# First layer's experts: three of four batches sorted by expert into blocks of 128 rows

## The chip, the cores and the metric

The kernel runs on one core of a Trainium2 chip. The metric is the time on the device in microseconds (us). The engines are called by the profile's names: PE (TensorE's matmuls, PEld its weight loads), DVE (VectorE), ACT (ScalarE), POOL (GpSimd) and SP (SyncE, which issues DMAs here).

## The reference, cut to what matters

Two layers, each an attention-like part and an expert part with gated residuals. What the change touches is the expert part of the first layer, on 4 batches of 1024 tokens of 128 values:

```python
E, FFN, TOP_K = 8, 176, 2
scores = softmax(xt @ gate_w.T)
topk_w, topk_idx = top_k(scores, TOP_K)
topk_w = topk_w / (sum(topk_w) + 1e-20)
combine = zeros((T, E)); combine[t, topk_idx] = topk_w
for e in range(E):
    g, u = split(xt @ w1[e], 2, axis=-1)
    out = out + combine[:, e:e + 1] * (silu(g) * u @ w2[e])
```

So each token needs two of eight experts; the reference computes all eight and weights six of them with zero.

## The kernel before

The program is a sequence of blocks: attention (16 groups, one for each batch and key head), the first layer's experts, a selective scan, and the second layer's experts with slots of a fixed capacity. A block ends for all engines together, and its last output is needed by the next block's normalization.

`experts` follows one list of steps, made by `experts_plan` (from line 1287 on); each engine walks through the same list and takes from it what is its own, so the list is the order of every queue. The 4096 tokens lie in 8 chunks of 512, and the 8 x 176 = 1408 hidden columns in 11 pieces of 128 (`NC`). One unit ("up", k) is a chunk and a piece: on PE six float32r matmuls of 512 columns (high and low parts, lines 1475 to 1477, for both halves of w1) and one that spreads the combine weights over the piece's rows (line 1484); on ACT a silu (1717), on DVE two products (1633, 1638). The step ("down", k) stands two units later (`LAG`) and adds four fp32 matmuls of 128 columns (1494), each of which the trace shows as two records. So all eight experts are computed for every token, and the combine weights, transposed and spread, do the choosing. A chunk's result is scaled by DVE (1647), added by POOL (1765) and its row statistics are taken by DVE.

Between the units stand the steps of preparation: "norm" (POOL), "ln" (transposes on PE, ACT), "score" (PE, 1442), "route" and "weights" (some twenty short DVE operations each, from 1511 and 1543 on), "tr" (the combine weights' transposes), "w" (the split of w1 into parts, in batch 0's first units), and steps for the next layer ("mod", "norm2", "ln2", "tap"). Ahead of the first unit are the output projection of attention's last batch ("out", 1414) and the routing of chunk 0. SP loads the weights at the start of the block.

The second layer's experts, `capacity_experts`, already send token rows to slots in memory (an indirect DMA from POOL, 1251), fetch them (SP, 2622), store results (2627) and gather them back (POOL, 2594); its gathers use four semaphores for each of the two choices.

Of the kernel before, what the change touches and what calls it, by code (L numbers as in the profile page):

```python
# [7 lines left out]
F32 = mybir.dt.float32  # L8
F32R = mybir.dt.float32r
I32 = mybir.dt.int32  # L10
# [445 lines left out]
def attention(nc, sems, a, h_t, attn_t, wo, ident, eps, zeros, stats, mv, mod_t, gates, slots_in, slots_zero):  # L456
# [3 lines left out]
    with ExitStack() as ctx:  # L460
# [526 lines left out]
        def sync(e):  # L987
# [6 lines left out]
            for step in plan:  # L994
# [30 lines left out]
                elif kind == "v" and key[0] in (1, 2):  # L1025
# [3 lines left out]
                                zeros[:, :, :].to_broadcast([P, E1 * CAPACITY // P, HID])).then_inc(slots_zero, 16)  # L1029
# [244 lines left out]
PHASES = ((0, 1), (1, 4), (4, NCHUNK))  # L1274


NORMED_AT = {1: (0, 0), 2: (0, 2), 3: (0, 4), 4: (1, 1), 5: (1, 6), 6: (2, 1), 7: (2, 6)}
CHOSEN_AT = {1: (0, 6), 2: (3, 1)}
MOD_AT = ((4, 2), (4, 5), (5, 2))

NEXT_AT = (((4, 4), (4, 7)), ((4, 9), (5, 3)))


def experts_plan():


    behind = {}

    def put(n, c, *steps):
        behind.setdefault(n * NC + c, []).extend(steps)  # L1290

    for n, (m, c) in NORMED_AT.items():
        put(m, c, ("norm", n))
        put(m, c + 1, ("ln", n))
        put(m, c + 2, ("score", n))
    for p, (m, c) in CHOSEN_AT.items():
        put(m, c, ("route", p))
        put(m, c + 1, ("rstd", 1) if p == 1 else ("rstd2",), ("exp", p))
        put(m, c + 2, ("weights", p))
    for n in range(1, NCHUNK):  # L1300
        put(n - 1, NC - 2, ("tr", n))
    for j, (m, c) in enumerate(MOD_AT):
        put(m, c, ("mod", j))
    for n, (rows_at, columns_at) in enumerate(NEXT_AT):
        put(*rows_at, ("norm2", n))
        put(*columns_at, ("ln2", n))
    put(NCHUNK - 1, 4, ("tap", 0))
    for c in range(NC - 3):
        put(0, c, ("w", c + 3))
# [3 lines left out]
    for k in range(NCHUNK * NC):  # L1313
        plan.append(("up", k))
        if k >= LAG:
            plan.append(("down", k - LAG))
        if k % NC == LAG + 1 and k > NC:
            plan.append(("stats", k // NC - 1))
        plan += behind.get(k, [])
    plan += [("down", k) for k in range(NCHUNK * NC - LAG, NCHUNK * NC)]  # L1320
    plan.append(("stats", NCHUNK - 1))
# [3 lines left out]
def experts(nc, sems, a, x, x_again, attn_t, wo, stats, mv, mod_t, gates, gate, iota, ident, eps, slots_zero, h_t, later, later_in,  # L1325
# [1448 lines left out]
```

## Time and profile before

| | us |
|---|---|
| median of 3 runs | 1877.63 (1877.07 to 1878.2) |
| profiled execution | 1874.3 |
| its span in the trace | 1872.6 |
| PE busy | 1552.5 (83% of the span) |
| DVE busy | 1187.0 (63%) |
| POOL busy | 1264.9 (68%) |
| ACT busy | 791.1 (42%) |

All times of rows are us from the start of the span. Busy shares are averages over stages with different limits, so they don't tell what a change in one stage is worth: that is read from stretches of that stage and from its timeline. A matmul's duration in a row is the time until its result is out, and matmuls overlap, so a rate is read from the distance between starts. The clock column is the granted clock of PE as a share of 2.4 GHz, where 1.00 is 2.4 and 0.50 is 1.2 GHz.

### The profile page before, as it was taken

The page shows a single profiled execution, that of the slowest core. Times are in us where ns is not written, and L with a number is a line of the kernel's source. Part 1 is how long each engine was busy: PE and PEld are TensorE (multiplying, and loading weights), DVE is VectorE, ACT ScalarE, POOL GpSimd, SP SyncE. Part 2 cuts the span into 40 slices and gives each one's busy share as a digit, 9 for nine tenths or more (in the row PEclk, how much of TensorE's full clock was granted, in tenths as well). Part 3 has the DMA queues.
Part 4 walks back from the last instruction along what each step waited for, and adds up shares of the span by engine and source line. Part 5 has one row for each costly group of instructions (what it writes and reads, how often), then busy time and mean ns, then how long its engine had stood idle before and what let it go on. Part 6 is the DMA issues. An engine that isn't in the chain of part 4 may idle for free. (4 is left out here: it accounts for less than half of the span.)

```text
span 1872.6 us, 26570 instructions
## 1 busy us (share of the span) xinstructions
PE 1552.5 (83%) x8882; PEld 1072.4 (57%) x8882; DVE 1187.0 (63%) x2509; ACT 791.1 (42%) x1347; POOL 1264.9 (68%) x1073
## 2 busy tenths in 40 slices
PE   5799999999999999999999989999965664356970
PEld 3455556755656765567656568888831231235970
DVE  6866676576666567666666235576659989952134
ACT  2245444344443354443444433322267855423320
POOL 5588998798888788887888753110026667658476
PEclk7799999999999999999999999999978876667995
DMA  6333322221122122122121020000036555405333
GB/s 176 70 80 79 69 56 47 46 68 35 40 63 69 29 52 68 35 52 63 35 58 45 12 67 1 1 1 1 1 101 157 143 124 139 115 26 173 98 93 85
DMA packets 93560, 125.30 MB, mean 67 GB/s; under 512 B 13664, under 2 KB 53492, under 8 KB 93424
## 3 DMA queue, kind: packets, MB, share of 16 engines
q1 hardware_dynamic: 89328, 115.58, 24.9%
q0 software_dynamic: 4096, 8.02, 1.5%
q8 instruction: 72, 1.18, 0.3%
q14 instruction: 64, 0.52, 0.1%
HBM read 56.56 MB, written 16.78 MB: 39 GB/s over the span
## 5 line engine op out<-in xcount | busy, mean ns | idle before, releaser
L838 DVE CUSTOM_DVE_ANT_0 ring<-ring,mask 128x128 f32<-128x128 f32 (+7 forms) x512 | 383.7, 769 | 186.0 <-PE ring L700 185.6
L924 ACT ACTIVATE prob<-ring 128x512 f32<-128x512 f32 x576 | 315.1, 597 | 296.6 <-PE ring L715 293.0
L978 POOL TENSOR_TENSOR acc<-acc,prob 128x512 f32<-128x512 f32 x272 | 353.3, 1299 | 72.1 <-ACT prob L924 48.3
L731 PE MATMUL ps_o<-prob,v 128*64 128x256 f32 x2304 | 282.0, 386 | 4.2 <-issue 3.8
L700 PE MATMUL ring<-k,x 128*128 128x512 f32 (+3 forms) x768 | 250.0, 405 | 36.4 <-ACT prob L924 22.1
L714 PE MATMUL ring<-x,k 128*128 128x512 f32 x576 | 258.6, 449 | 24.5 <-DVE neg_m L838 15.4
L715 PE MATMUL ring<-x,k 128*128 128x512 f32 x576 | 229.2, 398 | 0.0
L700 PEld LDWEIGHTS ring<-k,x 128*128 128x128 f32 x768 | 136.6, 197 | 143.9 <-ACT prob L924 50.5
L731 PEld LDWEIGHTS ps_o<-prob,v 128*64 128x64 f32 x2304 | 154.2, 137 | 106.3 <-issue 38.5
L975 POOL TENSOR_TENSOR acc<-prob 128x512 f32<-128x512 f32 x144 | 184.4, 1281 | 8.8 <-ACT prob L924 7.4
L945 POOL TENSOR_TENSOR other<-other,sin 128x512 f32<-128x512 f32 x96 | 136.3, 1420 | 57.1 <-DVE other L817 56.6
L714 PEld LDWEIGHTS ring<-x,k 128*128 128x128 f32 x576 | 109.3, 190 | 99.4 <-issue 44.0
L2375 POOL TENSOR_TENSOR m_hc<-m_st,m_crep 128x1024 f32<-128x1024 f32 x42 | 98.8, 2353 | 53.6 <-DVE m_st L2140 47.9
L947 POOL TENSOR_TENSOR rot<-rot,other 128x512 f32<-128x512 f32 x96 | 129.1, 1344 | 7.5
L1765 POOL TENSOR_TENSOR first_h<-first_h,e_scaled 128x512 f32<-128x512 f32 x8 | 10.3, 1285 | 174.4 <-DVE e_scaled L1647 174.4
L715 PEld LDWEIGHTS ring<-x,k 128*128 128x128 f32 x576 | 110.0, 191 | 19.9 <-issue 7.3
L830 DVE TENSOR_TENSOR rot<-rot,other 128x512 fp32r<-128x512 f32 x64 | 73.2, 1143 | 69.5 <-ACT other L906 69.5
L1633 DVE TENSOR_TENSOR e_both<-e_silu,ps_moe 128x512 f32<-128x512 f32 x88 | 60.4, 687 | 87.9 <-PE ps_moe L1477 69.4
L1717 ACT ACTIVATE e_silu<-ps_moe 128x512 f32<-128x512 f32 x88 | 52.6, 598 | 134.9 <-PE ps_moe L1477 132.2
L963 POOL TENSOR_SCALAR_AFFINE_SELECT prob<-prob 128x512 f32<-128x512 f32 x128 | 91.4, 714 | 25.8 <-ACT prob L924 24.7
L816 DVE TENSOR_TENSOR rot<-ring,cos 128x512 f32<-128x512 f32 x96 | 66.3, 690 | 58.1 <-PE ring L682 57.7
L2594 POOL DMA_INDIRECT c_got<-slots_out,f_slot x64 | 66.5, 1040 | 45.7 <-issue 39.8
(322 smaller groups left out, 3068.5 us busy)
## 6 DMA issues: line engine op xcount, KB each, us to landing
x<-other SPq DMA_DIRECT2D x256, 128.0 KB, 2.3
m_x_rep<-u_mem SPq DMA_DIRECT2D x59, 512.0 KB, 4.6
x<-rot SPq DMA_DIRECT2D x128, 128.0 KB, 2.3
slots_in<-zeros SPq DMA_DIRECT2D x2, 2048.0 KB, 8.7
slots_out<-wo SPq DMA_DIRECT2D x16, 256.0 KB, 2.5
gate<-slots_in SPq DMA_DIRECT2D x11, 256.0 KB, 3.2
m_x_rep<-u_mem SPq DMA_DIRECT2D x10, 256.0 KB, 4.2
e_w<-in_w SPq DMA_DIRECT2D x3, 704.0 KB, 6.9
```

The source lines that it names most:

```text
L700: mm = e.matmul(ps[:, c0:c1], x1[g % 2][:, h, qs], k1[g % 3][:, c0:c1], start=True, stop=True)
L714: e.matmul(banks(step, BANK), k1[g % 3][:, ks], x1[g % 2][:, :, qs], start=True, stop=False)
L715: e.matmul(banks(step, BANK), k2[g % 3][:, ks], x2[g % 2][:, :, qs], start=False, stop=True).then_inc(s2_pe.sem, 1)
L731: mm = e.matmul(ps_o[s * D:(s + 1) * D, qb % 2 * 2 * P:(qb % 2 + 1) * 2 * P], v[g % 2][:, kb, :], prob[i % NPROB][:, s * 2 * P:(s + 1) * 2 ...
L838: e.tensor_tensor_reduce(ps, ps, mask_1[:, SEQ - n:SEQ], 1.0, -3.0 * NEG, ALU.add, ALU.min, neg_m[g % 2][:, c, h, qb % QPC:qb % QPC + 1]). ...
L924: e.activation(prob[i % NPROB][:, :], banks(("s2",) + key, BANK), ACT.Exp, scale=-1.0).then_inc(s2_exp.sem, 1)
L945: e.tensor_tensor(other[i][:, :], other[i][:, :], sin[:, cc], ALU.mult).then_inc(rotated.sem, 1)
L947: e.tensor_tensor(rot[i][:, :], rot[i][:, :], other[i][:, :], ALU.add).then_inc(rotated.sem, 1)
L963: e.affine_select(tile[:, :], tile[:, :], [[0, G], [1, P]], ALU.is_ge, 0.0, base=0, channel_multiplier=-1).then_inc(causal.sem, 1)
L975: e.tensor_tensor(total[:, :], first[:, :], tile[:, :], ALU.add).then_inc(summed.sem, 1)
L978: e.tensor_tensor(total[:, :], total[:, :], tile[:, :], ALU.add).then_inc(summed.sem, 1)
L2375: e.tensor_tensor(hc[(b * NG + g) % NHC][:, :], st[r][:, :], crep[b % 2][:, :], ALU.mult).then_inc(hc_pool.sem, 1)
```

## The change

Batch 0 stays as it is: 22 units. Batches 1 to 3 are computed by choice of expert:

- For each of these batches DVE counts the tokens of each expert, PE forms running counts ("rank"), and DVE computes for both choices of every token a slot so that each expert's tokens start at a multiple of 128 ("place"), and a table with the expert of each of 24 blocks of 128 rows (`NBLOCK` = 16 + 8, enough for any distribution).
- PE loads the table's 24 values into registers ("regs"); the plan holds this step four times, twice for batch 2.
- The normalized rows are transposed back to token order ("back"), stored with the token's weight as a 129th value, and sent by POOL to their slots in memory, 16 indirect DMAs a batch ("send").
- SP fetches sets of 512 sorted rows; PE transposes them ("xt"), ACT and DVE split them. A step ("sup", q) computes a pair of blocks: for each block three float32r matmuls whose stationary side is the 128 rows and whose moving side is the 2 x 176 columns of the block's expert, at an address from a register. ACT takes the silu, DVE multiplies with weight and other half, PE transposes ("htr"), ACT copies, and "dn" multiplies by the expert's w2, again at a register's address. DVE scales, SP stores.
- POOL gathers each token's two results by indirect DMAs that add into x, 16 a batch, the second choice after the first eight have landed.
- In attention SP writes zeros to the three buffers of sorted rows. The wait for the gate's weights also covers a table and a constant, one of them issued behind the other weights.
- The final stage's gathers have two semaphores for each choice instead of four, since semaphores are short.

```diff
+                elif kind == "v" and key[0] in (3, 4, 5):
+
+                    e.dma_start(sorted_in[key[0] - 3].rearrange("(s p) n -> p s n", p=P),
+                                zeros[:, :, :].to_broadcast([P, NBLOCK, HID + 1])).then_inc(slots_zero, 16)
...
+DENSE = SEQ // BANK
+UNITS0 = DENSE * NC
+NBLOCK = 2 * TPB + E0
+SETS, PAIRS = NBLOCK // 4, NBLOCK // 2
...
+PHASES = ((0, 1), (1, 2), (2, 4), (4, 6), (6, 8))
...
+CHOSEN_AT = {1: 2, 2: 7, 3: 12}
...
+        if p >= 2:
+            put(k + 2, ("count", p - 1))
+            put(k + 3, ("rank", p - 1))
+            put(k + 4, ("place", p - 1))
+            put(k + 6, ("regs", p - 1))
...
+    for m, k in enumerate((12, 14, 17, 19)):
+        put(k, ("send", 1, 2 * m), ("send", 1, 2 * m + 1))
+    put(21, ("send", 2, 0), ("send", 2, 1))
+    for m, q in enumerate((1, 4, 7)):
+        put_among(q, ("send", 2, 2 * m + 2), ("send", 2, 2 * m + 3))
+    for m, q in enumerate((9, 12, 15, 17)):
+        put_among(q, ("send", 3, 2 * m), ("send", 3, 2 * m + 1))
...
+    put_among(4, ("score", 7), ("back", 7), ("stats", 1), ("mod", 0))
+    put_among(5, ("route", 4), ("exp", 4))
+    put_among(6, ("weights", 4), ("count", 3), ("rank", 3), ("place", 3))
+    put_among(8, ("regs", 2), ("mod", 1))
+    put_among(10, ("mod", 2))
...
+    put_among(19, ("regs", 3))
+    put_among(28, ("tap", 0))
+    for m, q in enumerate((20, 23, 26, 29)):
+        put_among(q, ("gather", 1, m))
+    for m, q in enumerate((32, 35)):
+        put_among(q, ("gather", 2, m))
...
+    plan.append(("xt", 0))
+    for q in range(pairs):
+        plan.append(("sup", q))
+        if q < 2:
+            plan.append(("down", UNITS0 - LAG + q))
+        if q % 2 and q + 1 < pairs:
+            plan.append(("xt", q // 2 + 1))
+        if q >= 1:
+            plan.append(("htr", q - 1))
+        if q >= 2:
+            plan.append(("dn", q - 2))
+        plan += among.get(q, [])
+        if q == 31:
+            plan.append(("sum", 1))
+    plan += [("htr", pairs - 1), ("dn", pairs - 2), ("dn", pairs - 1)]
+    plan += [("gather", 2, 2), ("gather", 2, 3), ("sum", 2)]
+    plan += [("gather", 3, m) for m in range(4)] + [("sum", 3)]
...
+                elif kind == "regs":
+                    b = step[1]
+                    e.wait_ge(placed, placed0 + b)
+                    _, expert[b] = nc.values_load_multi_w_load_instructions(
+                        of[0:1, b - 1, :], engines=[mybir.EngineType.PE], min_val=0, max_val=(E0 - 1) * F0,
...
+                elif kind == "xt":
+                    e.wait_ge(*rows_had(k))
+                    for j in range(4):
+                        mm = e.transpose(bank[:, j * P:(j + 1) * P], rows_of(k)[:, j, 0:HID], ident[:, :])
+                    mm.then_inc(xt_pe, 1)
+                elif kind == "sup":
+                    q = step[1]
+                    b, block, i = q // PAIRS + 1, 2 * (q % PAIRS), q // 2 % 2
+                    if q % 2 == 0:
+                        e.wait_ge(xt_dve, xt_dve0 + q // 2 + 1)
+                    if q < 2:
+                        e.wait_ge(both_dve, UNITS0 - 1 + q)
+                    else:
+                        e.wait_ge(hid_dve, UNITS0 + q - 1)
+                    for j in range(2):
+                        cols, to = slice((2 * (q % 2) + j) * P, (2 * (q % 2) + j + 1) * P), ps_up[q % 2][:, j, 0:2 * F0]
+                        at = bass.ds(expert[b][block + j], F0)
+                        e.matmul(to, xt_hi[i][:, cols], w_hi[:, :, at], start=True, stop=False)
+                        e.matmul(to, xt_hi[i][:, cols], w_lo[:, :, at], start=False, stop=False)
+                        mm = e.matmul(to, xt_lo[i][:, cols], w_hi[:, :, at], start=False, stop=True)
+                    mm.then_inc(up1_pe, 1)
+                elif kind == "htr":
+                    e.wait_ge(hid_dve, UNITS0 + k + 1)
+                    for j in range(4):
+                        mm = e.transpose(bank[0:HALF, j * P:(j + 1) * P], both[k % 2][:, j * HALF:(j + 1) * HALF], ident[:, :])
+                    mm.then_inc(htr_pe, 1)
+                elif kind == "dn":
+                    q = step[1]
+                    b, block = q // PAIRS + 1, 2 * (q % PAIRS)
+                    e.wait_ge(ht_act, q + 1)
+                    e.wait_ge(scale_dve, DENSE + q)
+                    for j in range(2):
+                        at, to = bass.ds(expert[b][block + j], HID), ps_dn[:, 2 * (q % 2) + j, :]
+                        for m in range(2):
+                            mm = e.matmul(to, hid[q % 2][0:HALF, (2 * j + m) * P:(2 * j + m + 1) * P], w2s[0:HALF, m, at], start=m == 0, stop=m == 1)
+                    mm.then_inc(dn_pe, 1)
...
+                elif kind == "xt":
+                    n = step[1]
+                    e.wait_ge(xt_act, xt_act0 + n + 1)
+                    e.tensor_tensor(xt_lo[n % 2][:, :], ps_c[turn[step] % 2], xt_hi[n % 2][:, :].bitcast(F32), ALU.subtract).then_inc(xt_dve, 1)
+                elif kind == "sup":
+                    q = step[1]
+                    e.wait_ge(silu_act, UNITS0 + q + 1)
+                    if q >= 2:
+                        e.wait_ge(htr_pe, q - 1)
+                    for j in range(2):
+                        cols = slice(j * F0, (j + 1) * F0)
+                        t = e.scalar_tensor_tensor(both[q % 2][:, cols], silu[q % 2][:, cols], rows_of(q // 2)[:, 2 * (q % 2) + j, HID:HID + 1],
+                                                   ps_up[q % 2][:, j, F0:2 * F0], ALU.mult, ALU.mult)
+                    t.then_inc(hid_dve, 1)
+                elif kind == "dn":
+                    q = step[1]
+                    b, n = q // PAIRS + 1, q // 2
+                    e.wait_ge(dn_pe, UNITS0 + q + 1)
+                    if n >= 2:
+                        e.wait_ge(res_out[n % 2][0], res_out[n % 2][1] + n // 2 * 16)
+                    half = slice(2 * (q % 2), 2 * (q % 2) + 2)
+                    e.tensor_tensor(hid[2 + n % 2][:, :].rearrange("p (j n) -> p j n", n=HID)[:, half, :], ps_dn[:, half, :],
+                                    gates[0][1][:, b:b + 1, :].to_broadcast([P, 2, HID]), ALU.mult).then_inc(scale_dve, 1)
...
+                if kind == "send":
+                    _, b, i = step
+                    if i % 2 == 0:
+                        e.wait_ge(up1_pe, begun)
+                    if i == 0:
+                        e.wait_ge(placed, placed0 + b)
+                        e.wait_ge(tok_act, tok0 + 4 * b)
+                        if b > 2:
+                            e.wait_ge(*all_sent(b - 2))
+                    for k in range(2):
+                        e.indirect_dma_start(sorted_in[b - 1][:, :], bass.IndirectOffsetOnAxis(ap=slot[:, b - 1, k * TPB + i:k * TPB + i + 1], axis=0),
+                                             tok[b % 2][k][:, i, :], None, bounds_check=NBLOCK * P - 1, oob_is_err=False).then_inc(sent[b % 2], 16)
+                elif kind == "gather":
+                    _, b, m = step
+                    if begun < UNITS0 + pairs - 1:
+                        e.wait_ge(up1_pe, begun)
+                    if m == 0:
+                        for r, base in res_out:
+                            e.wait_ge(r, base + b * SETS // 2 * 16)
+                    if m == 0 and b > 2:
+                        e.wait_ge(got[b % 2], (b - 1) // 2 * 2 * TPB * 16)
+                    if m == 2:
+                        e.wait_ge(got[b % 2], ((b - 1) // 2 * 2 + 1) * TPB * 16)
+                    for i in range(4 * (m % 2), 4 * (m % 2) + 4):
+                        e.indirect_dma_start(x[:, b * TPB + i, :], None, sorted_out[b - 1][:, :],
+                                             bass.IndirectOffsetOnAxis(ap=slot[:, b - 1, m // 2 * TPB + i:m // 2 * TPB + i + 1], axis=0),
+                                             bounds_check=NBLOCK * P - 1, oob_is_err=True, compute_op=ALU.add).then_inc(got[b % 2], 16)
...
+            for j in range(2):
+                e.dma_start(w2s[0:HALF, j, :].rearrange("p (e f) -> p e f", f=F0)[:, :, 0:HID],
+                            a["w2_0"][:, j * HALF:(j + 1) * HALF, :].rearrange("e p n -> p e n")).then_inc(w2_in, 16)
+            e.dma_start(blocks[:, :], a["blocks"][0:1, :]).then_inc(gate_in, 16)
...
+            def fetch(n):
+                b, at = n // SETS + 1, n % SETS * BANK
+                if n % SETS == 0:
+                    e.wait_ge(*all_sent(b))
+                if n >= 3:
+                    e.wait_ge(hid_dve, UNITS0 + 2 * n - 4)
+                    e.wait_ge(xt_pe, xt_pe0 + n - 2)
+                e.dma_start(rows_of(n)[:, :, :], sorted_in[b - 1][at:at + BANK, :].rearrange("(s p) n -> p s n", p=P)).then_inc(sorted_done[n % 3][0], 16)
+
+            def store(n):
+                b, at = n // SETS + 1, n % SETS * BANK
+                e.wait_ge(scale_dve, DENSE + 2 * n + 2)
+                e.dma_start(sorted_out[b - 1][at:at + BANK, :].rearrange("(s p) n -> p s n", p=P),
+                            hid[2 + n % 2][:, :].rearrange("p (j n) -> p j n", n=HID)).then_inc(res_out[n % 2][0], 16)
+            sets = (BATCH - 1) * SETS
+            for n in range(2):
+                fetch(n)
+            for n in range(sets):
+                if n + 2 < sets:
+                    fetch(n + 2)
+                store(n)
...
-        gathered0, gathered1 = ([sem(f"gather{k}_{m}") for m in range(4)] for k in range(2))
+        gathered0, gathered1 = ([sem(f"gather{k}_{m}") for m in range(2)] for k in range(2))
```

## Rows read from the trace of the kernel before

**Rows 1.** Stretches: start:end, length, busy us (instructions) by engine, clock, DMA.
```profile
1113.20:1181.60 68.40, 62.34 (x387) 54.58 (x386) 40.02 (x96) 28.71 (x51) 23.81 (x36) 1.00 0.00 1
1181.60:1365.90 184.30, 178.91 (x1093) 156.82 (x1092) 114.13 (x226) 49.94 (x82) 17.17 (x25) 1.00 0.00 1
```

**Rows 2.** Timeline: start, duration, engine, line, tiles, [idle before, releaser].
```profile
1290.47 0.48 PE L1475 MATMUL ps_moe<-e_h_hi,e_w1hi 128*128 128x512 f32 x1
...
1291.72 0.40 PE L1477 MATMUL ps_moe<-e_h_hi,e_w1lo 128*128 128x512 f32 x1
...
1292.19 1.05 PE L1494 MATMUL ps_moe<-e_w,e_hid 128*128 128x128 f32 x8
1293.00 0.48 PE L1475 MATMUL ps_moe<-e_h_hi,e_w1hi 128*128 128x512 f32 x1
...
1292.22 0.69 DVE L1633 TENSOR_TENSOR e_both<-e_silu,ps_moe 128x512 f32<-128x512 f32 x1 [0.94 <-PE ps_moe L1477]
```

**Rows 3.** Timeline, the first up matmul of batch 0.
```profile
1113.25 0.48 PE L1475 MATMUL ps_moe<-e_h_hi,e_w1hi 128*128 128x512 f32 x1
```

**Rows 4.** Timeline of PE, the first unit of batch 1.
```profile
1181.11 0.48 PE L1475 MATMUL ps_moe<-e_h_hi,e_w1hi 128*128 128x512 f32 x1
```

**Rows 5.** Timeline of DVE, end of the stage and start of the next.
```profile
1365.11 0.69 DVE L1647 TENSOR_TENSOR e_scaled<-ps_moe,gate 128x512 f32<-128x512 f32 x1 [1.43 <-PE ps_moe L1494]
...
1368.77 1.33 DVE L2145 COPY m_w_b<-m_w_x 128x128 f32<-128x128 f32 x1 [0.32 <-PEq L1781]
```

**Rows 6.** Timeline: four transposes' loads, eight narrow matmuls, four 16-column loads.
```profile
1103.11 0.47 PEld L1423 LDWEIGHTS ps_moe<-ident,e_xn 128*128 128x128 f32 x4
...
1104.78 1.03 PE L1442 MATMUL ps_route<-gate,e_h 128*128 128x8 f32 x8 [0.96 <-ACT e_h L1691]
...
1112.78 0.42 PEld L1447 LDWEIGHTS ps_moe<-ident,e_comb 128*16 128x16 f32 x4
```

**Rows 7.** The line of the two zero fills in attention.
```profile
L1028 SPq DMA_DIRECT2D slots_in<-zeros x2: 442/442/443, 105.3 to 170.6; - x2
...
DMA to landing us min/median/max: 8.7/8.7/8.7
```

**Rows 8.** The line of the final stage's fetches: issue to landing.
```profile
DMA to landing us min/median/max: 2.7/3.3/4.5
```

**Rows 9.** The line of the final stage's gathers: POOL's register moves, min/median/max ns.
```profile
L2594 POOLq MOVE  x64: 29/29/29, 1767.0 to 1846.1; - x64
```

**Rows 10.** The line of a small load issued behind w1 and w2.
```profile
L1777 SPq DMA_DIRECT2D e_ct<-in_c_t x1: 2624/2624/2624, 1098.5 to 1098.5; - x1
...
DMA to landing us min/median/max: 7.5/7.5/7.5
```

**Rows 11.** Timeline of DVE, the first two operations of one routing.
```profile
1105.85 0.19 DVE L1511 TENSOR_REDUCE e_best<-ps_route 128x4 f32<-128x32 f32 x1 [1.67 <-PE ps_route L1442]
1106.08 0.19 DVE L1513 TENSOR_TENSOR e_less<-ps_route,e_best 128x32 f32<-128x32 f32 x1
```

**Rows 12.** Timeline of POOL, one of the final stage's sends.
```profile
1716.08 0.97 POOL L1251 DMA_INDIRECT slots_in<-attn_t,f_slot  x1 [0.30 <-issue]
```

**Rows 13.** Timeline of POOL, a gather; the DMA view's line of all gathers.
```profile
1777.11 1.00 POOL L2594 DMA_INDIRECT c_got<-slots_out,f_slot  x1 [0.31 <-issue]
...
c_got<-slots_out,f_slot POOLq DMA_INDIRECT x64, 2.6
```

**Rows 14.** Stretches of attention, about one group each.
```profile
170.00:236.00 66.00, 62.51 (x365) 40.20 (x362) 42.91 (x95) 29.53 (x56) 58.06 (x49) 1.00 0.32 81
236.00:301.00 65.00, 60.98 (x358) 39.70 (x357) 42.92 (x96) 29.15 (x55) 58.41 (x50) 1.00 0.22 49
```

**Rows 15.** Stretches of the next stage; a 512-column matmul's load at low clock.
```profile
1440.00:1460.00 20.00, 9.85 (x38) 3.31 (x31) 18.52 (x22) 13.72 (x21) 12.91 (x6) 0.67 0.56 135
1460.00:1480.00 20.00, 16.84 (x71) 8.38 (x69) 19.93 (x37) 16.53 (x17) 13.27 (x8) 0.93 0.58 155
...
1374.42 0.19 PEld L2046 LDWEIGHTS m_ps_w<-attn_t,w_tap 128*128 128x128 f32 x1 [0.24 <-issue]
```

More of the change, by code:

```diff
@@ L1316, in experts_plan, with experts @@
             plan.append(("down", k - LAG))
-        if k % NC == LAG + 1 and k > NC:
-            plan.append(("stats", k // NC - 1))
+        if k == NC + LAG + 1:
+            plan.append(("stats", 0))
         plan += behind.get(k, [])
-    plan += [("down", k) for k in range(NCHUNK * NC - LAG, NCHUNK * NC)]
-    plan.append(("stats", NCHUNK - 1))
+    pairs = (BATCH - 1) * PAIRS
+    plan.append(("xt", 0))
[15 more added lines that the diff above has]
+    plan += [("gather", 3, m) for m in range(4)] + [("sum", 3)]
     return plan
-def experts(nc, sems, a, x, x_again, attn_t, wo, stats, mv, mod_t, gates, gate, iota, ident, eps, slots_zero, h_t, later, later_in,
+def experts(nc, sems, a, x, x_again, attn_t, wo, stats, mv, mod_t, gates, gate, iota, ident, eps, slots_zero, sorted_in, sorted_out, marks, past, h_t, later, later_in,
             cw, w_in, w_tap):
     plan = experts_plan()
-    spare = [step for step in plan if step[0] in ("out", "ln", "tr", "up", "mod", "ln2", "tap")]
+    spare = [step for step in plan if step[0] in ("out", "ln", "tr", "up", "mod", "ln2", "tap", "back", "rank", "xt", "htr")]
     turn = {step: i for i, step in enumerate(spare)}
     shift, scale = 3, 4
+    pairs = (BATCH - 1) * PAIRS
     with ExitStack() as ctx:
@@ L1359, in experts @@
         scaled = [sb(f"scaled{i}", [P, 4, HID]) for i in range(2)]
+        xt_hi, xt_lo = ([sb(f"xt_{n}{i}", [P, BANK], F32R) for i in range(2)] for n in ("hi", "lo"))
+        sorted_rows = [sb(f"sorted{i}", [P, 4, HID + 1]) for i in range(3)]
+        w2s = sb("w2s", [P, 2, E0 * F0])
+        room = attn_t[:, :, :, :].rearrange("p k j n -> p (k j n)")[:, 2 * SEQ:2 * SEQ + 4 * TPB * (HID + 1)]
+        tok = [[room[:, (2 * i + j) * TPB * (HID + 1):(2 * i + j + 1) * TPB * (HID + 1)].rearrange("p (t n) -> p t n", n=HID + 1)
+                for j in range(2)] for i in range(2)]
+        tri, ones, less_one = sb("tri", [P, P]), sb("ones", [P, P]), sb("less_one", [P, P])
+        both_masks, upto, keep, pos = (sb(n, [P, E0, TPB]) for n in ("both_masks", "upto", "keep", "pos"))
+        steps, one, need, end, start = (sb(n, [P, E0]) for n in ("steps", "one", "need", "end", "start"))
+        more, picked, slot_f = sb("more", [P, E0, E0]), sb("picked", [P, 2 * TPB, E0]), sb("slot_f", [P, 2 * TPB])
+        slot = sb("slot", [P, BATCH - 1, 2 * TPB], I32)
+        blocks, over, of_f = sb("blocks", [1, NBLOCK]), sb("over", [1, NBLOCK, E0]), sb("of_f", [1, NBLOCK])
+        of = sb("of", [1, BATCH - 1, NBLOCK], I32)
         ct, sct, wm = sb("ct", [P, BATCH]), sb("sct", [P, BATCH]), sb("wm", [P, 6 * HID])
@@ L1744, in gpsimd @@
                     t.then_inc(norm2_pool, 1)
-                elif kind == "ln":
+                elif kind == "ln" and step[1] < DENSE:
                     n = step[1]
```

247 lines of the change are left out of this document (194 added, 53 removed).

## The prediction

> **What bounds the kernel now.** I read the busy times by stretch first, to find the stage and the engine that sets its pace; then the timeline of one unit; then the stage's entry and exit; then the final stage, because it already has the kinds of transfer that the change adds. In the stretches [rows 1] the experts of the first layer run from 1113.2 to 1368.7. TensorE (PE) is busy 62.3 of 68.4 us and then 178.9 of 184.3 us at a granted clock of 1.00, DVE 62% and GpSimd (POOL) 9% of the second stretch: PE is the bound there, and what is saved on PE shortens the span. One unit (128 of the 1408 hidden columns for 512 tokens) takes 2.52 us in steady state, from 1290.47 to 1293.00: seven 512-column matmuls 0.23 apart (1291.72 to 1292.19 holds two) and eight records of the down step in 0.81 [rows 2]. Batch 0's 22 units begin at 1113.25 and the first unit of batch 1 at 1181.11 [rows 3, 4]; the next block's first work on DVE is at 1368.77 [rows 5]. So 67.9 us stay and 187.7 us are replaced.
>
> **What PE does instead.** Each later batch becomes 24 blocks of 128 rows, 12 pairs, 36 pairs in all. One pair needs 6 up matmuls of 352 columns: 0.23 x 352/512 = 0.16, and since not all of the 0.23 shrinks with the columns 0.166, together 1.00. It needs 4 transposes of the hidden rows and, once in two pairs, 4 of the input; four transposes take 0.47, as in [rows 6], so 0.70. The down step has 4 fp32 matmuls, 8 records at 0.118 (a quarter of the 0.47) = 0.94. Sum 2.65 us a pair if PE waits for nothing, 95 us for 36.
>
> **What sets the pace of a pair.** The rows make a round trip through memory, and SyncE's loop ties it to PE: the fetch of set n+2 stands behind the store of set n-1, which waits for the scaled result of pair 2n-1. From the end of that pair's down step: 0.5 for DVE's scaling (half of a 0.69 op and its wait), 0.45 for issuing the store (0.44 in [rows 7]), 3.3 until the fetch lands [rows 8], so 4.25. PE meanwhile does 2.4 + 1.0 = 3.4 and stands at the transposes of set n+2. After these come 1.9 of PE work until the next such down step, so the loop closes in 6.1 us, 6.3 with the copy and subtraction on ScalarE and DVE: 3.15 us a pair. Bounds: 2.65 (fetch early enough) and 4.0 (below). DVE needs 0.68 + 0.35 + 0.42 plus gaps = 1.6 a pair from its 0.69 per 512 columns [rows 2], ScalarE 1.4; neither binds.
>
> **Register addresses.** The column offset of each expert comes from a PE register; the trace shows no such matmul. Ten of them stand in a pair. A register MOVE on POOL's queue takes 0.029 [rows 9], a whole DMA issue on SyncE 0.44 [rows 7]. With one or two register operations for each, the added time lies between 0.3 and, at 0.1 for each matmul and repeated for each record, 1.4 us. Records with a 16-column load and those with an 8-column moving side both stay at 0.11 to 0.12 apart [rows 6], which looks like the sequencer's own rate, so such operations may not be hidden. The fetch leaves 0.4 a pair of PE idle to hide them; I take 0.3, hence nothing on top of 3.15.
>
> **Loading the registers.** 24 loads, then the same again for the second and third batch, and the plan loads the second batch's twice: four times. At 0.029 a load this is 0.7 us each time, at 0.44 it is 10.6. I take 0.12, near the geometric middle, 2.9 each time, and 1 us of it under matmuls already queued: 4 us in the dense phase, 3 in the sorted one, whose waits hide some. Everything behind it on PE waits, and so DVE and ScalarE. The Trainium skill (Runtime: NRT & Kernel Launch, section Instruction fetch mechanics) gives about 200 ns per register loaded, even in bulk; no run here shows it yet. By that price an estimate is 4.8 us a time and the sum some 7 us more.
>
> **Entry, +3.5.** The wait on the gate's semaphore now asks for four transfers, and the fourth is issued behind w1, w2 and the second copy of w2 (0.72 MB). Before, the small transfer issued behind w2 landed at 1098.49 + 7.5 = 1106.0 while the scores began at 1104.78 [rows 6, 10]. The added 0.72 MB take 2.1 to 2.9 us at 250 to 340 GB/s, so the scores start at about 1108.3. They stand ahead of the second output projection on PE, so all of it counts; bounds 2 and 5.
>
> **Dense phase, +2.8 and +1.** On PE: four transposes back (1.9) and two rank products (1.4), less one transpose (0.4). DVE gets routing and placing for three batches, about 24 us of short operations at 0.22 each, as [rows 11] show, where 22 units leave it 26. They come in bursts of 3 to 6 us, and PE runs ahead of DVE by about 1.9, so most are hidden; 1 us for the rest (bounds -2, since the 2.0 us wait for the combine weights goes, and 6).
>
> **Start of the sorted phase, +5.** The last four sends wait for unit 19, take 0.97 + 0.30 each on POOL [rows 12] and land about 3 later; then the fetch 3.3, transposes 0.5, copy 0.6, subtraction 0.7, while PE has 2.9 units left. The two last down steps are queued behind. Bounds 2 and 8.
>
> **Within it.** 32 pairs at 3.15 are 100.8. DVE's burst at pairs 4 to 6 (routing, counting, placing, about 10 us) exceeds the 1.6 spare a pair plus 1.5 of lead by 4. Scores, transposes and the modulation of the next layer are 7 us of PE, 3 of them uncovered; registers 3. So pair 32 begins at 1181.1 + 3.5 + 3.8 + 4 + 5 + 100.8 + 10 = 1308.2.
>
> **The tail.** PE ends about 15 later. From pair 32 POOL gathers batch 2: 16 indirect DMAs 1.30 apart (1.00 and 0.31 ahead of it) [rows 13], with one landing (2.6) between the halves that add into the same rows: 23.4. Batch 3's 16, 2 landings and the statistics follow: 20.8 + 5.9 + 2.6, then 0.3 for the block's end. With 1 us for accumulation, which the trace does not show, 54 us after pair 32 begins: 1362.2, against 1368.7 (the 1368.77 of [rows 5]). In these last 38 us PE is idle; before, 3.7, from the scaling at 1365.11 on.
>
> **Outside the stage.** Three zero fills of 1.6 MB enter SyncE's queue in attention. The two of 2 MB that are there land in 8.7 and the group periods around them are 65 to 66 us with and without [rows 7, 14], so 0 (bounds 0 and 3). At the end half as many semaphores let eight gathers fly instead of sixteen; a group's landing (2.6) lies under the four issues (5.2) of the next [rows 13], so 0.
>
> **Sum.** 1362.2 - 1368.7 = -6.5; I round to -6. The profiled execution took 1874.3 (span 1872.6), 3.3 below the median 1877.6; so 1868 for a profiled one and 1871.6 for the median.
>
> **Rivals.** (1) The work is PE-bound and registers are cheap: pairs at 2.75 and loads at 0.7 save 13 + 5 us more, 1854. For it: PE needs 2.65, and a fetch landed in 2.7 at best. Against it: the store-before-fetch order. (2) PE's sequencer becomes the bound, the case on the other side: register operations ahead of ten matmuls a pair, at the 0.11 per record that is perhaps already its rate, make a pair 3.8 instead of 3.15, 36 x 0.65 = 23 us more: 1895. It decides from 3.32 us a pair, where the 6 us are gone. (3) Register loads at 0.44 cost 4 x 10.6 instead of 7, with cover some 30 more: 1902. (4) The clock falls: in the next stage, where PE is busy for half to 0.84 of the time, the grant is 0.67 to 0.93 and 512-column matmuls stand 0.43 apart (0.19 and 0.24) [rows 15] instead of 0.23. At that ratio a pair takes 4.9 and the stage 63 more, 1935; half of it, 1903, if it falls in part. For it is that six of sixteen PE steps a pair are transposes; against it, the clock was 1.00 through the first stretch with 9% idle [rows 1]. The skill (TensorE: Matmul & The Clock Gate, section Part 4) says that transposes don't count as PE activity; by it the rival would win, and the trace has no stretch of this mixture to agree or not. (5) The change does not do what it says: 24 blocks are a fixed number, run whether filled or not, so the saving can't fail through the data; I give it 0.
>
> **How the numbers follow.** Forecast 0.46 (1862 to 1881), rival 1 0.14, rival 2 0.22, rival 3 0.11, rival 4 0.05, others 0.02. What a measurement of this kernel can tell from no change is about 0.2%, 3.7 us. Of the forecast's 0.46, 0.32 lies below 1873.9, 0.10 within the band and 0.04 above. Faster: 0.32 + 0.14 + 0.01 = 0.47. Same: 0.10 + 0.02 from rival 2 = 0.12. Slower 0.41. The range runs from 1848, rival 1 with its cheaper bounds, to 1906, which takes in rivals 2 and 3 and leaves rival 4's worse half out.
>
> **What would show it.** Starts of the up matmuls of the sorted phase two pairs apart by 6.3, with PE waiting ahead of the input transposes for a DMA: right. No such wait and gaps named issue: rival 2. A gap on PE of over 3 us ahead of units 14 and 19 and pairs 9 and 20: the loads. Scores at 1108.3; POOL issuing gathers 1.30 apart for 38 us after PE's last matmul; granted clock 1.00 up to there. I am wrong most easily in the pair: each 0.1 us is 3.6.

## The result and the profile after

The changed kernel takes 1904.8 us (median of 4 runs, 1904.5 to 1907.4), the kernel before 1877.35 beside it: ratio 1.0151, 95% interval 1.0133 to 1.0168. The change costs 27.5 us where I forecast a gain of 6. The profiled execution has a span of 1905.7 us, 33.1 more than before.

In stretches (start:end, length, busy us and instructions of PE, PE's loads, DVE, ScalarE, POOL, then clock, DMA share, GB/s), the dense units of batch 0, the 36 pairs, and what comes behind PE's last matmul; they answer to [rows 1]:

```profile
1124.10:1204.10 80.00, 68.12 (x408) 59.07 (x407) 52.94 (x160) 35.42 (x60) 38.58 (x54) 0.96 0.05 15
1204.10:1345.60 141.50, 115.20 (x821) 106.35 (x819) 70.49 (x201) 57.59 (x105) 73.31 (x68) 0.95 0.38 92
1345.60:1399.00 53.40, 0.00 (x0) 0.00 (x0) 4.57 (x32) 0.00 (x0) 37.33 (x24) 0.53 0.26 35
```

PE's busy time fell from 241 to 183 us, but PE now stands still for 12 us in the first stretch, 26 in the second, and all of the third. The waits of PE from 1105 to 1345.6 (engine, tile, line <- who ended the wait: us in all, times, longest):

```profile
PE ps_moe L1562 <- DMA e_sorted<-sorted_in: 11.0, 11, 1.9
PE ps_moe L1550 <- DVE e_upto L1730: 7.3, 2, 5.1
PE ps_route L1540 <- DMA e_blocks<-in_blocks: 6.4, 1, 6.4
PE ps_moe L1576 <- DVE e_xt_lo L1835: 5.0, 13, 1.5
PE ps_moe L1521 <- DVE e_of L1765: 3.3, 1, 3.3
...
PE ps_moe L1635 <- DVE e_of L1765: 2.3, 1, 2.3
```

Four mechanisms are named there: the fetch of the sorted rows (L1562 are the input's transposes), DVE's counting and placing (L1550 is the rank product), the block numbers, and the copy and subtraction behind the transposes.

*Entry* (timeline; answers to [rows 3, 6, 10]):

```profile
1100.64 5.48 SPq L2081 DMA_DIRECT2D e_w2s<-in_w  x2
1106.16 0.41 SPq L2083 DMA_DIRECT2D e_blocks<-in_blocks  x1
1111.94 1.88 PE L1540 MATMUL ps_route<-gate,e_h 128*128 128x8 f32 x8 [6.38 <-DMA e_blocks<-in_blocks]
1113.67 6.50 PE L1512 MATMUL ps_moe<-wo,attn_t 128*128 128x128 f32 x30
1124.15 0.48 PE L1626 MATMUL ps_moe<-e_h_hi,e_w1hi 128*128 128x512 f32 x1
```

SyncE needs 5.48 us to issue the two loads of w2's second copy, so the 24 block numbers are issued only at 1106.16, and PE goes on 5.8 later. The DMA engines are full all the while: from 1100 to 1112 their share, the last number but one, is 1.06.

```profile
1100.00:1112.00 12.00, 5.62 (x51) 5.39 (x50) 1.42 (x7) 2.02 (x4) 0.02 (x1) 0.90 1.06 267
```

The eight narrow score matmuls then take 1.88 us, where [rows 6] have 1.03: PE's clock had fallen while it waited (granted 0.61 from 1112 to 1122). The first expert matmul starts at 1124.15 instead of 1113.25.

*Two undisturbed pairs* (timeline; releaser in brackets):

```profile
1301.24 0.63 PE L1562 MATMUL ps_moe<-ident,e_sorted 128*128 128x128 f32 x4 [0.30 <-DMA e_sorted<-sorted_in]
1303.36 0.42 PE L1576 MATMUL ps_moe<-e_w1hi,e_xt_hi 128*128 x1 [0.16 <-DVE e_xt_lo L1835]
1303.68 0.36 SPq L2100 DMA_DIRECT2D sorted_out<-e_hid  x1
1304.14 0.45 SPq L2095 DMA_DIRECT2D e_sorted<-sorted_in  x1
1305.68 0.41 PE L1576 MATMUL ps_moe<-e_w1hi,e_xt_hi 128*128 x1
1307.43 0.63 PE L1562 MATMUL ps_moe<-ident,e_sorted 128*128 128x128 f32 x4 [0.54 <-DMA e_sorted<-sorted_in]
1309.56 0.42 PE L1576 MATMUL ps_moe<-e_w1hi,e_xt_hi 128*128 x1 [0.17 <-DVE e_xt_lo L1835]
```

From 1303.36 to 1309.56 two pairs take 6.2 us, and PE waits ahead of the input's transposes for the fetch that stands behind the store. Pairs 0, 12, 32 and 34 begin at 1208.19, 1262.65, 1330.14 and 1336.57.

*Tail* (timeline; answers to [rows 5]):

```profile
1388.76 1.56 POOL L2027 DMA_INDIRECT first_h<-sorted_out,e_slot  x1 [0.30 <-issue]
1390.63 1.56 POOL L2027 DMA_INDIRECT first_h<-sorted_out,e_slot  x1 [0.30 <-issue]
1394.01 1.64 DVE L156 BATCH_NORM_STATS2 stats<-first_h 128x6 f32<-128x128 f32 x8 [29.85 <-DMA first_h<-sorted_out,e_slot]
1395.68 0.64 DVE L160 BATCH_NORM_AGGREGATE mv<-stats 128x2 f32<-128x6 f32 x8
1399.07 1.34 DVE L2474 COPY m_w_b<-m_w_x 128x128 f32<-128x128 f32 x1 [2.74 <-PEq L2110]
```

A gather that adds into its rows takes 1.56 us and the next comes 1.86 behind it, not 1.30 as in [rows 13]. The next block's DVE work, at 1368.77 before, starts at 1399.07: 30.3 of the 33.1 us.

### The profile page after: what moved, and what is told of

The parts are those of the page before. It is cut to its first block and busy times, and to the rows that moved or that the text cites. A ratio compares the mean times of both kernels' runs of the same rounds, so it can differ in the third digit from the quotient of the medians.

```text
span 1905.7 us, 26684 instructions
## 1 busy us (share of the span) xinstructions
PE 1500.2 (79%) x8630; PEld 1028.2 (54%) x8630; DVE 1158.4 (61%) x2573; ACT 805.4 (42%) x1379; POOL 1375.1 (72%) x1162
## 5 line engine op out<-in xcount | busy, mean ns | idle before, releaser
L2027 POOL DMA_INDIRECT first_h<-sorted_out,e_slot x48 | 74.9, 1561 | 33.7 <-PE ps_moe L1578 13.7
L743 PE MATMUL ps_l<-acc,v_one 128*64 128x256 f32 x576 | 87.2, 380 | 2.9 <-POOL acc L978 2.9
L1255 POOL DMA_INDIRECT slots_in<-attn_t,f_slot x64 | 63.7, 995 | 32.9 <-issue 14.9
```

## The experiments

Ratios are to the kernel before, run beside each. The changed kernel's is 1.0151 (1.0133 to 1.0168); marks in a trace are more exact for single steps.

**The entry.**

```diff
             e.dma_start(tri[:, :], a["tri"]).then_inc(gate_in, 16)
+            e.dma_start(blocks[:, :], a["blocks"][0:1, :]).then_inc(gate_in, 16)
...
-            e.dma_start(blocks[:, :], a["blocks"][0:1, :]).then_inc(gate_in, 16)
```

> The changed kernel with one transfer moved: the 24 block numbers are fetched right behind the triangle, ahead of w1, instead of behind both copies of w2. Theory A (the entry is set by the place in SyncE's queue: two issues of 2.8 us and 0.72 MB stand ahead of the block numbers, and while PE waits 6.4 us for them its clock falls, so the second output projection takes 10.3 us instead of 7.4): scores start near 1106.4 instead of 1111.9, the projection is back at 7.4, the first expert matmul comes 8 us earlier, median 1904.8 - 8 = 1897. Rival B (the transfers of w1 and w2 fill the DMA engines, and any small transfer lands late beside them, or the weights become the last wait): 0 to 3 us earlier, 1902 to 1905.

Measured: 1894.96 us, ratio 1.0089 (1.006 to 1.0118). Scores at 1107.13, the first expert matmul at 1115.60, 8.5 earlier, with the attention's end 0.7 later: behind it the entry is as long as in the kernel before (18.6 us). Theory A, as far as the place in the queue goes. The transfer now stands ahead of the loads' issues and of their bytes at once, so the run doesn't tell which of the two had made it late.

**Register addresses and loads.**

```diff
-                        at = bass.ds(expert[b][block + j], F0)
+                        fixed = min((block + j) // 3, E0 - 1) * F0
+                        at = slice(fixed, fixed + F0)
...
-                    _, expert[b] = nc.values_load_multi_w_load_instructions(of[0:1, b - 1, :], ...)
+                    expert[b] = None
```

> The changed kernel without register loads and register addresses: each block's matmuls read the columns of a fixed expert (blocks 3e to 3e+2 those of expert e), so the experts' results are not those asked for; all else stays, every wait and matmul included. Theory A (register addresses and loads are hidden: no gap stands at the loads in the dense phase, 0.8 us stands at one in the sorted phase): 0 to 3 us less, median 1902 to 1905. Rival B (the sequencer pays for each addressed matmul, as my second rival had it): 0.3 to 0.65 us less a pair, 11 to 23 less, 1882 to 1894. Rival C (the loads cost about 5 us a time): 10 to 20 less.

Measured: 1899.75 us, ratio 1.0127 (1.0097 to 1.0156). In the trace the step between an even pair and the next odd one, where PE waits for nothing, is 2.31 us with registers and 2.32 without: addressing costs nothing there. It does show where PE's sequencer has been held by a wait. One subtraction and the up matmul that it releases, in the changed kernel and then here:

```profile
1302.53 0.69 DVE L1835 TENSOR_TENSOR e_xt_lo<-ps_moe,e_xt_hi 128x512 fp32r<-128x512 f32 x1 [0.35 <-ACT e_xt_hi L1944]
1303.36 0.42 PE L1576 MATMUL ps_moe<-e_w1hi,e_xt_hi 128*128 x1 [0.16 <-DVE e_xt_lo L1835]
```

```profile
1298.77 0.69 DVE L1835 TENSOR_TENSOR e_xt_lo<-ps_moe,e_xt_hi 128x512 fp32r<-128x512 f32 x1 [0.62 <-ACT e_xt_hi L1944]
1299.51 0.43 PE L1575 MATMUL ps_moe<-e_w1hi,e_xt_hi 128*128 128x352 f32 x1
```

From the end of the subtraction it is 0.14 us with a register address and 0.05 without; over the 18 sets that is some 1.5 us. Where the table is loaded at pair 8 a step shrinks from 4.25 to 3.19. From pair 0 to 32 it gained 4.5 us in all; 1.0 of that is this load and some 1.5 are the addresses. The other 2 are less than the scatter: pairs 12 to 34 took 73.9, 74.0, 76.6 and 79.1 us in four kernels that are alike there, 71.5 here, and PE's waits for the fetch were no shorter (12.6 us against 11.0). What the trace of the changed kernel has for the addresses and loads:

```profile
L1556 PEldq TENSOR_LOAD <-e_of x3: 1689/1806/1964, 1175.7 to 1289.2; - x3
...
L1576 PEldq FUSED_REGOPS  x72: 37/42/42, 1208.1 to 1338.0; - x72
...
L1577 PEldq ALU_OP  x72: 32/32/42, 1208.2 to 1338.1; - x72
...
L1593 PEldq ALU_OP  x72: 32/32/32, 1216.8 to 1344.1; - x72
L1593 PEldq FUSED_REGOPS  x72: 46/51/51, 1216.9 to 1344.3; - x72
```

(Line, queue and operation, count, duration ns min/median/max, first and last start.) All 24 offsets come in one instruction of 1.8 us, three times in all.

> The changed kernel with each of its four steps that load 24 registers done four times over, 96 loads for 24. Theory A (the sequencer runs ahead of the matmuls queued and a load costs 0.03 to 0.05 us: where the step stands in pair 8 of the changed kernel a gap of 0.8 us is named issue, and none stands at units 13 and 18): the pair with the step at 8 grows by 3 us (72 more loads at 0.045), units 13 and 18 by at most 2.5, in all 5 to 9 us more. Rival B (my forecast's 0.12 a load): 8.6 a time, 25 to 35 more. Rival C (0.2 a load, as the Trainium skill has it in Runtime: NRT & Kernel Launch, section Instruction fetch mechanics; no row shows it): 14.4 a time, 50 or more.

The three repeats in front of the last one had no reader, and the built program doesn't contain them: its trace has three TENSOR_LOADs as well, and as many instructions, 26684. So this experiment measured nothing of a load; it is a second measurement of the changed kernel, 1901.6 us (two runs), ratio 1.0123 (1.0105 to 1.014), and shows how far two such measurements lie apart. It also shows that the plan's first load for batch 2, which is done again before use, is not in the program either.

**The gathers.**

```diff
-  bounds_check=NBLOCK * P - 1, oob_is_err=True, compute_op=ALU.add).then_inc(got[b % 2], 16)
+  bounds_check=NBLOCK * P - 1, oob_is_err=True).then_inc(got[b % 2], 16)
```

> The changed kernel with the gathers of the sorted results writing over the rows instead of adding into them (the sums are left out). Theory A (the accumulation is what makes a gather 1.56 us long instead of 1.00): the 24 gathers behind PE's last matmul come 1.30 apart instead of 1.86, 24 x 0.56 = 13.4 less, and 1 from the first half of batch 2: median 1890. Rival B (the length comes from the table read in memory or from where the rows are written): 1.86 apart still, 1905.

Measured: 1887.36 us, ratio 1.0044 (1.0027 to 1.006). Gathers in its trace, then in that of the changed kernel:

```profile
L2027 POOL DMA_INDIRECT first_h<-sorted_out,e_slot x48: 1004/1010/1065, 1283.3 to 1372.7; - x48
...
DMA to landing us min/median/max: 2.5/2.6/3.9
```

```profile
L2027 POOL DMA_INDIRECT first_h<-sorted_out,e_slot x48: 1548/1559/1657, 1287.3 to 1390.6; - x48
...
DMA to landing us min/median/max: 3.2/3.3/4.8
```

From pair 32 (1328.01) to the next block (1381.90) it took 53.9 us, against 68.9 in the changed kernel: the adding is 15 us of the tail. Theory A.

**SyncE's order.**

```diff
-            for n in range(2):
+            for n in range(3):
                 fetch(n)
             for n in range(sets):
-                if n + 2 < sets:
-                    fetch(n + 2)
+                if n + 3 < sets:
+                    fetch(n + 3)
                 store(n)
```

> The changed kernel with SyncE's order turned: the fetch of set n+3 is issued ahead of the store of set n (three fetches first) instead of behind it. Theory A (the loop of store, fetch and transposes makes two pairs 6.3 us where nothing disturbs them): PE's 11 waits ahead of the input transposes, 11.0 us in all, go; two undisturbed pairs take 5.5 to 5.7; from pair 12 to 34 that is 8 to 11 us less, median 1894 to 1897. Rival B (PE's own queue is the bound, through register addresses or through the chain of copy and subtraction behind the transposes): the waits turn into others, two pairs stay above 6.1, 0 to 3 us less.

Measured: 1892.45 us, ratio 1.0075 (1.0048 to 1.0101). Waits of PE from 1260 to 1345.6, of this kernel, then of the changed one:

```profile
PE ps_moe L1576 <- DVE e_xt_lo L1835: 2.2, 10, 0.3
PE ps_moe L1583 <- DVE gate L1786: 1.3, 1, 1.3
PE ps_moe L1593 <- DVE e_hid L1853: 0.7, 1, 0.7
PE ps_moe L1583 <- DVE e_both L1843: 0.5, 1, 0.5
```

```profile
PE ps_moe L1562 <- DMA e_sorted<-sorted_in: 9.4, 10, 1.9
PE ps_moe L1576 <- DVE e_xt_lo L1835: 2.4, 11, 0.8
```

The wait for the fetch is gone, two pairs take 5.5, and pairs 12 to 34 take 62.9 instead of 73.9. Theory A.

**DVE's bursts.** ScalarE copies the ranks out (a copy of 72 columns and a semaphore), and the plan shifts:

```diff
-            put(k + 3, ("rank", p - 1))
-            put(k + 4, ("place", p - 1))
+            put(k + 4, ("rank", p - 1))
+            put(k + 5, ("place", p - 1))
...
-    put_among(6, ("weights", 4), ("count", 3), ("rank", 3), ("place", 3))
+    put_among(6, ("weights", 4), ("count", 3))
+    put_among(7, ("rank", 3), ("place", 3))
```

> The changed kernel with the ranks kept out of PE's way: ScalarE copies them from their bank at once, so that the bank is free before DVE has placed the rows; PE takes the rank products one step later than the routing; and the first of the two loads of batch 2's registers is dropped. Theory A (PE waits behind DVE's bursts: 3.3 and 2.3 us for the bank, 2.2 and 5.1 us for the counts, and its clock falls behind the longest of them): those waits shrink from 12.9 to under 4, another 2 us come from the clock, median 10 lower than the changed kernel, 0.5 point in the ratio. Rival B (DVE's work itself is late, whoever waits for it: the bursts then hold PE at the hidden rows instead): 0 to 3 us lower.

Measured: 1897.35 us, ratio 1.0094 (1.0079 to 1.0109). From the first expert matmul to the last replicating one of the dense units it takes 73.7 us instead of 78.9, from pair 0 to 12 50.1 instead of 54.5: 9.6 together. The start of the sorted phase takes 2.0 of that back, and pairs 12 to 34 took 79.1, with PE's waits for the fetch at 17.7 us; how much of these 5 is scatter I can't tell. Of the four waits behind the bursts (12.9 us) one of 1.9 is left, in front of a rank product: theory A. A new gap of 2.8 us, named issue, stands ahead of unit 14, where the register load now comes right behind the placing.

**Two parts of the change alone, in the kernel before.** The final stage with two semaphores for each choice's gathers instead of four, and the three zero fills in the attention stage:

> The kernel before with one part of the change alone: in the final stage the gathers count on two semaphores for each choice instead of four, so that group m waits for the landing of group m-2. Theory A (my forecast: a group's landing lies under the issues of the next): no change, ratio 1.000. Rival B (the final stage of the changed kernel is 2.3 us longer from its first to its last gather, and this is its price): 2 to 3 us slower, ratio 1.0012 to 1.0016.

> The kernel before with another part of the change alone: the three zero fills of 1.6 MB in the attention stage, to which the first layer's weights wait as they do in the changed kernel. Theory A (my forecast: hidden): no change, ratio 1.000. Rival B (the changed kernel's attention ends 1.7 us later, and the fills are why): 1 to 2 us slower, ratio 1.0005 to 1.001, the last output projection at 1096.3 instead of 1094.6.

Measured: 1877.21 us, ratio 0.9993 (0.9984 to 1.0002), and 1874.8 us, 0.9986 (0.9977 to 0.9994). Neither costs anything. The 1.7 us by which the changed kernel's attention ended late lie within the scatter: the last output projections begin between 1094.5 and 1098.0 in the twelve traces with its attention stage (at 1096.5 in this one with the fills, as rival B had it, but its time is not longer), and at 1095.5 in the kernel with the two semaphores, whose attention is that of before.

**Gathers earlier**: batch 1's at pairs 18, 20, 22, 24, batch 2's at 27, 29, 31, 33.

> The changed kernel with the gathers put earlier into the plan: batch 1's at pairs 18, 20, 22, 24 instead of 20, 23, 26, 29, batch 2's at 27 to 33 instead of 32, 35 and behind the end. Theory A (POOL's row of gathers is what ends last, and it starts too late): the first gather at pair 18, then 48 gathers at 1.86 with five landings of 2.5 without a break; batch 2 is in by 1348 instead of 1363, the stage ends 12 us earlier, median 1893. Rival B (gathers and fetches share the DMA engines, and more gathers beside the pairs make the fetches land later): PE's waits for the fetch grow from 11 us to some 20, half of the gain is given back, 1898.

Measured: 1894.76 us, ratio 1.0092 (1.0075 to 1.0109). The last gather starts at 1379.63 instead of 1390.63. PE's waits for the fetch are 13.2 us instead of 11.0 and pairs 12 to 34 take 2.3 more, which is inside their scatter: theory A, and B is not shown.

**Together, and with the adding taken off the gathers.** The second kernel gathers into the two token buffers, and DVE adds:

```diff
+                elif kind == "add":
+                    _, b, k = step
+                    e.wait_ge(got[k], b * TPB * 16)
+                    if b > 1 or k:
+                        e.wait_ge(added, 2 * (b - 1) + k)
+                    tiles = x[:, b * TPB:(b + 1) * TPB, :]
+                    e.tensor_tensor(tiles, tiles, tok[b % 2][k][:, :, 0:HID], ALU.add).then_inc(added, 1)
```

> The changed kernel with the four corrections that keep its work together: block numbers first, fetch of set n+3 ahead of the store of set n, ranks copied out and a step later, gathers of batches 1 and 2 early. Theory A (with PE out of the way the row of 48 gathers that add, 1.86 apart, with its landings, 105 us from pair 18, ends the stage): first expert matmul at 1115.6, pair 18 at 1265, next block at 1375 instead of 1399, median 1880, ratio 1.001. Rival B (the four gains of 8, 11, 10 and 12 us add up): 1864, ratio 0.992.

> As the one before, but the gathers write the two expert results of a row into two buffers of their own, which the tokens no longer need, and DVE adds them to the rows (two adds of 1024 columns a batch); the wait between the halves of a batch is gone. Theory A (without the accumulation a gather takes 1.00, the row of them keeps up with the pairs, and behind the last store only batch 3's 16 gathers at 1.31 stand, 21 us, with a landing, two adds and the statistics): next block at 1351, median 1857, ratio 0.989. Rival B (DVE's adds, 2.7 us a batch, and the gathers beside the fetches slow the pairs by 0.3 us each): 1868, ratio 0.995.

Measured: 1874.14 us, ratio 0.9984 (0.9974 to 0.9993), and 1855.44 us, ratio 0.9879 (0.9862 to 0.9895). In the first PE is through by 1315.4, and the row of gathers, 1262.24 to 1356.70, ends the stage; it took 94 us where I had counted 105, and the next block begins at 1365.14: theory A, only shorter. In the second the gathers of batches 1 and 2 are through by 1312 and only batch 3's sixteen stand behind the last store; the next block begins at 1351.2. Its last lines:

```profile
1342.02 1.01 POOL L2045 DMA_INDIRECT attn_t<-sorted_out,e_slot  x1 [0.30 <-issue]
1344.61 1.23 DVE L1866 TENSOR_TENSOR first_h<-first_h,attn_t 128x1024 f32<-128x1024 f32 x1 [9.21 <-DMA attn_t<-sorted_out,e_slot]
1345.87 1.64 DVE L156 BATCH_NORM_STATS2 stats<-first_h 128x6 f32<-128x128 f32 x8
```

This is theory A again, and it beats the kernel before by 22 us and the changed one by some 49. The last try was to load batch 1's table two units later:

> As the kernel with the gathers apart, but batch 1's table of 24 expert offsets is loaded behind unit 15 instead of unit 13. In that kernel, and in the one with the ranks copied, PE stands 2.8 us ahead of unit 14, named issue, with the load (1.8 us for 24 registers in one instruction) behind DVE's placing in front of it. Theory A (the load costs nothing when matmuls are queued behind which it can run, and 2.8 when PE's sequencer has to wait for the placing first): the gap is gone, unit 14 follows unit 13 by 2.5 instead of 5.6 us, median 3 lower, 1852.5, ratio 0.9862. Rival B (any load drains PE's queue for its 1.8 us): the gap moves to unit 16, no change, 0.9879.

Measured: 1856.13 us, ratio 0.9883 (0.9866 to 0.9899), no different. The gap named issue is gone, so the load had been uncovered there and is covered here. But units 14 and 15 stand 4.6 us apart now, 1.8 of it waiting for DVE, which is in its next burst, and the clock falls behind that wait (0.50 from 1167.3 to 1170.3): from unit 13 to 17 it takes 14.5 us, as with the load in its old place. So the gap had stood where PE, without it, waits for DVE. Neither theory saw that. The dense units are 1.5 us shorter all the same, but elsewhere, between units 2 and 3. PE waits 2.41 us for DVE in front of unit 2 in both kernels; behind it the clock fell in the kernel with the gathers apart and stayed in this one:

```profile
1122.00:1125.00 3.00, 3.00 (x11) 2.45 (x9) 0.91 (x2) 2.50 (x5) 1.03 (x1) 0.52 0.00 0
```

```profile
1120.80:1123.80 3.00, 3.00 (x23) 2.69 (x20) 1.27 (x3) 2.50 (x5) 1.22 (x1) 1.00 0.00 0
```

## Why the prediction was wrong

Its sign was wrong, the time at the upper end of its range. The forecast put the profiled span at 1866.1; it is 1905.7, and the 39.6 us lie like this (dense units: unit 21 starts at 1201.61, and 2.52 later is 1204.1):

| step | forecast | measured | miss |
|---|---|---|---|
| first expert matmul | 1116.75 | 1124.15 | +7.4 |
| dense units | 67.9 + 3.8 + 4 | 80.0 | +4.3 |
| start of the sorted phase | 5 | 4.1 | -0.9 |
| pairs 0 to 32 | 100.8 + 10 | 121.95 | +11.1 |
| pair 32 to the next block | 54 | 68.9 | +14.9 |
| all behind | 503.8 | 506.6 | +2.8 |

**The tail** is the largest miss and a mis-sized term: "with 1 us for accumulation, which the trace does not show". It was 0.56 for each of the 32 gathers behind pair 32. I gave no bounds to the one operation of which no row existed, though it stood 32 times in a row on the path that sets the end. Without the adding, the tail measured 53.9, the forecast's 54.

**The pair.** The loop was right: two undisturbed pairs take 6.2, against 6.3, and turning SyncE's order gives 2.75 a pair. But 3.15 was taken as the mean, and it is near the least: from pair 12 to 34 two pairs take 5.9 to 8.2 us. A fetch lands in 2.9 to 4.5 us (median 3.6), its wait is in series with the loop, and so lateness is never made up: pairs 12 to 34 average 3.36. The load of batch 3's table and the tap's products fall in here too.

**DVE's bursts.** "PE runs ahead of DVE by about 1.9, so most are hidden; 1 us for the rest" failed in a way that the plan could have shown: the rank product stands in PE's queue right behind the counting on DVE, and holds a spare bank until DVE has placed the rows. PE can't run ahead past either. The waits are 12.9 us in four places. In the sorted phase one place alone takes more than the 4 us: pair 7 begins 8.9 behind pair 6, 5.8 more than a pair's 3.15, and pairs 0 to 12 are 16.7 over twelve times 3.15. Behind the waits PE's clock falls:

```profile
1170.00:1175.00 5.00, 5.00 (x24) 4.43 (x24) 1.58 (x3) 1.38 (x2) 0.00 (x0) 0.66 0.00 0
...
1240.00:1246.00 6.00, 5.53 (x22) 5.04 (x23) 3.96 (x16) 1.24 (x3) 0.00 (x0) 0.50 0.02 5
```

The granted clock is 0.50 from 1240 to 1246, the lower of PE's two levels, after the 5.1 us wait, and 0.66 from 1170 to 1175, after 3.3. So a long wait can be paid again in the matmuls behind it: at the entry the second output projection took 10.3 us instead of 7.4.

**The entry.** Forecast +3.5, measured +9.2 behind an attention that ended 1.7 later. The scores came 5.5 later behind it, 2.0 over the forecast, and from the scores to the first expert matmul it took 12.2 us instead of 8.5: these 3.7 are the lower clock behind the wait of 6.4, a term that the forecast had at nothing. I priced the added loads by their bytes alone (0.72 MB, 2.1 to 2.9 us). SyncE took 5.5 us to issue them, and behind that the small transfer still needed 5.8 until PE went on, with the DMA engines full; whether issue or bytes made the 2.0 stays open. The long issue is not a matter of bytes or rows alone either: in [rows 10] a transfer of 2 KB took 2.62 us to issue, and 1.03 in the changed kernel.

**Registers.** Here the forecast was too dear, as were rivals 2 and 3, which carried most of my chance for slower. A pair has 0.31 us of register operations (twice 0.042 + 0.032 for the up step and twice 0.032 + 0.051 for the down step), my 0.3. They are hidden but for 0.09 us where a wait stands in front of them, some 1.5 us in all. The loads are three, not four, 1.8 us each, not 2.9, and cost 0, 1.1 and next to nothing (under a wait for the fetch), instead of 7. The Trainium skill (Runtime: NRT & Kernel Launch, section Instruction fetch mechanics) has about 200 ns a register; here it is 1.81 / 24 = 0.075, and the measurement decides.

**The clock** (rival 4) did not fall with the mixture of work: it is 1.00 from 1263 to 1336, in pairs of which six in sixteen steps are transposes. The Trainium skill (TensorE: Matmul & The Clock Gate, section Part 4) says that transposes don't count as PE activity. I took from it that such a mixture would run at the lower clock; this one didn't. The falls stand behind idle waits, and once, from 1229 to 1232 at 0.50, behind 2.5 us of scores, transposes and products of 4 columns; there narrow products stand beside the transposes, so it doesn't tell which of them did it.

**Outside the stage**: zero fills and semaphores cost nothing, as forecast. The last +2.8 lies within the scatter: from the next block's start to the end the eleven traces with this final stage and the sorted experts take 502.4 to 506.7 us, around the 503.8 of before, and the row of 64 gathers in it takes 93.8 to 97.2.

What made the whole slower was none of my rivals: not one mechanism but four, each at the edge of the new work and worth 8 to 15 us when it is taken out: the entry, DVE's bursts, the fetch behind the store, and the adding of the gathers. PE's saving itself was there all the time, and with the four removed and the gathers of batches 1 and 2 moved forward it shows: 1855 us.

## What to carry to other kernels

When compute is traded for moving rows, count how often the new kind of transfer is issued in series behind the last matmul, and bound its price on both sides where no row has it. Loads issued ahead of a small transfer make it late, and the engine that waits for it can lose its clock on top, so what a gate waits for goes first, and a fetch goes ahead of a store that it doesn't depend on. A producer and its consumer in neighbouring steps of two in-order queues (the count on DVE, the rank on PE) stop the engine that runs ahead for the whole burst: put a step between them and free the bank early.

## What the hardware showed that I had not expected

- An indirect gather into SBUF that adds takes POOL 1.56 us for 128 rows of 128 values, one that writes 1.01; the landing is 3.3 against 2.6.
- One instruction loads 24 registers in 1.8 us, and matmuls already queued run on meanwhile: no gap where a unit's matmuls stand in the queue, 2.8 us where the load comes right behind the wait for its table.
- Issuing one of the two loads of w2's second copy (88 partitions, 8 experts, 352 KB) took SyncE 2.7 us, and one of 2 KB behind them 1.03 (2.62 in the kernel before), others beside it 0.43. No run here says why.
- Addresses of matmuls from registers: 32 to 51 ns for each operation in PE's sequencer, hidden behind weight loads of 0.19 us, and 0.09 us in front of the first matmul behind a wait.
- One and the same wait of 2.41 us was followed by PE's lower clock in one kernel (0.52) and not in another (1.00), so traces of kernels that are alike there differ by 1.5 us.
